# A transformer block on one core: first loads reordered, norms in pairs, the first probabilities turned amid the second scores, context tiles in the order of use

## The chip, the cores and the metric

The kernel runs on one core of one Trainium2 chip. Its engines are TensorE (PE), VectorE (DVE), ScalarE (ACT), GpSimd (POOL) and SyncE (SP), which here only issues DMA transfers. The metric is the device time of one execution in microseconds, the median of several runs.

## What is computed

The input `x` is 8 batches of 64 tokens with 512 channels; a context `ctx` has 512 rows of 512 for each batch. Three residual steps follow each other, each on a layer norm of `x`:

```python
x = x + xattn(layernorm(x), ctx)      # cross attention
x = x + attn(layernorm(x))            # delta rule, FIR filters, gates
x = x + ffn(layernorm(x))             # 8 routed experts (top 2) and 2 shared ones
```

The change touches the first step alone:

```python
def xattn(inputs, context):
    gate_signal = context @ Wg + bg
    attn = softmax(gate_signal @ inputs^T, over the context rows)
    return (attn^T @ context) @ Wo + bo
```

## The kernel before

Everything is float32. The 512 tokens are NT = 4 tiles of 128 tokens, two batches in each; the 512 channels are DC = 4 chunks of 128. The program is written by hand for each engine: what stands in an engine's block is its queue, in that order, and engines meet at semaphores (`wait_ge`). Nothing reorders it.

Instead of multiplying the context by `Wg`, the kernel multiplies the normed tokens by it (`transform`), so that the scores are one product of the transformed tokens with the turned context. `bg` then adds one number per token (`c0s`, VectorE's `tensor_tensor_reduce`), which the exponential's bias takes in.

**SP's queue** loads, in this order: `x[0]`, `consts` (identity, masks and small tables in one block), `x[1]` to `x[3]`, `wgT` (1 MB), `cols`, `rows`, `tickets`, `bgrow`, then for each tile the turned context `ctxT` (2 MB, for the scores) and the context `ctx` (2 MB, for the values), with `wox` (1 MB) after tile 1. All go through one DMA queue. Only then does SP wait, for the first turned values (`oT_done`), and loads `wqkv` over tile 0 of the ring.

**VectorE** does for each tile `begin_norm(t)` (statistics, mean and variance, variance plus eps; GpSimd then raises it to a power) and `end_norm(0, t)` (four small steps of a reciprocal root, and the write of `xn[t]`), interleaved: the beginning of tile t+1 comes before the end of tile t. Then come the four products for `c0s`, `keep_transform` (PSUM to `yT`), `x + bo`, and `score_bias` (maximum over a row of scores and two small steps).

**TensorE** waits for `consts`, runs two 512-column matmuls on them for warm-up (`keep_warm`, the result is not used), transposes tile 0 (`transpose_tile`, waits for `xn_ready`), runs a third, and then does `transform(0)` in two halves of 8 matmuls each around the transposes of tile 1; then a set of transposes and a transform of the tile before, in turn. Then come `scores(0)`, `scores(1)`, `turn_probs(0)` and, for each tile, `values`, `turn_probs` of the next, `project` of the one before, `scores` of the one after next, `turn_values`. One transform is 16 matmuls, one tile of scores or values 8, a set of transposes 4; each float32 matmul stands in the trace as two records.

**ScalarE** copies the transposed tiles to `xnT`, makes `exponentials(0)` and `exponentials(1)`, and then for each tile copies the turned probabilities from PSUM to `probsT_b` (`pT_ready`, which `values` waits for), makes the exponential of the next and scales the values.

After the cross attention come the projections `wqkv` of the second step (line 613 on). Its convolutions, FIR filters and delta rule take until about 240 us, and the experts the rest.

The lines that matter, in the profile's numbers: L499 warm-up, L512 transposes of the normed tile, L523 transform, L547 scores, L557 `turn_probs`, L569 values, L579 `turn_values`, L590 `project`, L613 the first projections; on VectorE L1371 to L1373 `begin_norm`, L1365 to L1368 the root, L1379 the write of `xn`, L1398 the products, L1392 `keep_transform`, L1415 to L1417 `score_bias`, L1427 the reciprocal in `normalise`, which waits for the exponential; on ScalarE L1080 the copy to `xnT`, L1090 the exponential, L1099 the copy of the turned probabilities, L1106 the values.

## Time and profile before

| what | us |
|---|---|
| median of 3 runs | 448.68 (448.63 to 451.23) |
| profiled execution | 448.59 |
| its span, first to last instruction | 446.8 |
| TensorE busy | 429.9 |
| VectorE busy | 307.0 |
| ScalarE busy | 175.5 |
| DMA | 92.41 MB, mean 207 GB/s |

The span is what the trace shows; the execution's own time is 1.8 us longer, for what lies around it. Times in the trace count from the span's start. Busy shares are a mean over stages with different limits; what ends a stage is read from the chain of waits, which follows the last instruction back to what released each step.

### The profile page before, as it was taken

Reading aid. Unit: us, or ns where it says so; the run is one execution under the profiler, and the core shown is the slowest. Engines: PE = TensorE matmul, PEld = TensorE weight load, DVE = VectorE, ACT = ScalarE, POOL = GpSimd, SP = SyncE. Lnnn points to the kernel's source line nnn. Section 1 sums busy time; section 2 is a strip of 40 time slices with the busy share of each in tenths; the row PEclk is TensorE's granted clock in tenths of the full one; section 3 lists DMA queues with packets and bytes.
Section 4 is the critical chain, followed back from the end, with each engine's and each line's share of the span. In section 5 each row is a group of like instructions: output and inputs, shape, how many; then the busy total and the mean of one; then the engine's idle time right before and its main releaser. Section 6 shows DMA issues by size and latency. Waiting matters only on the chain.

```text
span 446.8 us, 8180 instructions
## 1 busy us (share of the span) xinstructions
PE 429.9 (96%) x3184; PEld 287.5 (64%) x3184; DVE 307.0 (69%) x572; ACT 175.5 (39%) x235; POOL 73.8 (17%) x78
## 2 busy tenths in 40 slices
PE   5998999999999999999999999999999999999996
PEld 2953345744445756688865398884457788888872
DVE  5541235698889899886658966510475899999965
ACT  1102111387752211022223243110337778888730
POOL 1000000000023700228631100155100000000061
PEclk9999999999998999999779999999999999999999
DMA  8999959836212530065000200044989999999545
GB/s 318 433 428 425 425 244 321 266 92 187 102 32 94 161 91 9 4 266 208 3 0 0 96 0 2 24 166 85 269 305 389 347 373 412 377 397 396 223 135 170
DMA packets 17937, 92.41 MB, mean 207 GB/s; under 512 B 3424, under 2 KB 5104, under 8 KB 10736
## 3 DMA queue, kind: packets, MB, share of 16 engines
q1 hardware_dynamic: 14880, 78.82, 47.4%
q10 hardware_dynamic: 1488, 8.93, 5.8%
q0 software_dynamic: 1536, 4.20, 2.9%
q8 instruction: 23, 0.38, 0.3%
q14 instruction: 10, 0.08, 0.1%
HBM read 82.25 MB, written 12.08 MB: 211 GB/s over the span
## 4 chain that ended last, share of the span: by engine, by line
PE 82%; DVE 9%; SPq 2%; DMA 2%; issue 1%; ACT 1%; POOL 1%; DVEq 0%; ACTq 0%
PE bank L921 34%; PE bank L735 8%; PE bank L660 6%; PE bank L686 4%; PE bank L569 3%; PE bank L523 3%; PE bank L547 3%; PE bank L590 3%; PE bank L499 2%; SPq L333 2%; DVE part L1496 2%; PE bank L711 2%; PE bank L897 2%; DVE x L1712 1%; PE bank L712 1%
## 5 line engine op out<-in xcount | busy, mean ns | idle before, releaser
L1496 DVE SCALAR_TENSOR_TENSOR part<-ring,cols,part 128x504 f32<-128x504 f32 (+13 forms) x64 | 42.0, 715 | 0.1
L735 PEld LDWEIGHTS bank<-ring 64*64 64x64 f32 x960 | 33.4, 140 | 10.2 <-issue 8.8
L735 PE MATMUL bank<-ring 64*64 64x64 f32 (+1 forms) x960 | 37.8, 230 | 0.8 <-issue 0.7
L686 PE MATMUL bank<-xnT,ring 128*128 128x512 f32 (+1 forms) x96 | 37.7, 544 | 0.7 <-ACT xnT L1080 0.7
L427 POOL TENSOR_TENSOR small<-small 128x1 f32<-128x1 f32 (+2 forms) x12 | 12.1, 1005 | 134.6 <-DVE small L1373 73.6
L660 PE MATMUL bank<-early,ring 128*32 128x512 f32 (+15 forms) x512 | 33.3, 402 | 0.3 <-DVE early L1515 0.3
L1496 DVE SCALAR_TENSOR_TENSOR ring<-bank,cols,ring 128x504 f32<-128x504 f32 (+2 forms) x36 | 26.3, 733 | 5.1 <-ACT ring L1128 4.1
L686 PEld LDWEIGHTS bank<-xnT,ring 128*128 128x128 f32 x96 | 17.6, 190 | 17.2 <-issue 14.5
L1262 ACT ACTIVATE rows<-bank 128x512 f32<-128x512 f32 x19 | 11.4, 598 | 39.5 <-PE bank L921 39.5
L660 PEld LDWEIGHTS bank<-early,ring 128*32 128x32 f32 x512 | 14.5, 112 | 15.2 <-issue 11.2
L436 POOL TENSOR_TENSOR ring<-ring,consts 128x256 f32<-128x256 f32 x20 | 15.8, 815 | 46.8 <-DVE ring L1628 32.5
L1693 DVE TENSOR_TENSOR w1a<-early,w1a 128x2048 fp32r<-128x2048 f32 x7 | 16.0, 2288 | 10.3 <-issue 10.3
L1218 ACT ACTIVATE ring<-bank 128x256 f32<-128x256 f32 x20 | 7.7, 384 | 34.6 <-PE bank L735 34.0
L499 PE MATMUL bank<-consts 128*128 128x512 f32 x24 | 16.2, 801 | 4.8 <-DMA consts<-masks_in 4.8
L1768 DVE TENSOR_TENSOR hTa<-rows,bank 128x512 f32<-128x512 f32 x15 | 10.3, 687 | 13.0 <-PE bank L921 12.9
L486 POOL TENSOR_TENSOR small<-small 128x1 f32<-128x1 f32 x1 | 0.2, 195 | 111.1 <-DMA ys<-yout 111.1
L921 PE MATMUL bank<-xe,hTs 128*128 128x512 f32 x72 | 17.9, 398 | 0.6 <-DVE hTs L1867 0.6
L921 PE MATMUL bank<-w3a,xgT 128*128 128x512 f32 x72 | 18.0, 398 | 0.0
L1693 DVE TENSOR_TENSOR w3a<-early,w3a 128x2048 fp32r<-128x2048 f32 x7 | 16.0, 2287 | 2.8 <-ACT w3a L1194 2.8
L1194 ACT ACTIVATE w1a<-early 128x2048 fp32r<-128x2048 f32 x7 | 13.4, 1908 | 11.2 <-DMA early<-wffn_in 11.2
L921 PE MATMUL bank<-w1a,xgT 128*128 128x512 f32 x72 | 17.5, 392 | 0.0
L569 PE MATMUL bank<-ring,early 128*64 128x512 f32 x64 | 14.6, 599 | 1.9 <-ACT early L1099 1.9
(256 smaller groups left out, 903.5 us busy)
## 6 DMA issues: line engine op xcount, KB each, us to landing
early<-wffn_in SPq DMA_DIRECT2D x21, 1024.0 KB, 7.4
ring<-ctxT_in SPq DMA_DIRECT2D x4, 2048.0 KB, 26.3
ring<-ctx_in SPq DMA_DIRECT2D x4, 2048.0 KB, 30.7
raw1b<-wffn_in SPq DMA_DIRECT2D x6, 1024.0 KB, 9.8
raw3b<-wffn_in SPq DMA_DIRECT2D x6, 1024.0 KB, 8.9
raw2b<-wffn_in SPq DMA_DIRECT2D x6, 1024.0 KB, 7.9
ring<-firw_in SPq DMA_DIRECT2D x4, 1024.0 KB, 4.9
xs<-zeros_in ACTq DMA_DIRECT2D x1, 3840.0 KB, 13.9
```

Of the source, the lines that this page charges most:

```text
L436: pool.tensor_tensor(by_tile(lts[l][:, h]), by_tile(mt[:, h]), spread_half(HF_L1 + 1 + l), ALU.mult).then_inc(S["lt_ready"], 1)
L499: pe.matmul(dst, ident, consts[:, 0:512], start=True, stop=True)
L523: last = pe.matmul(bank[2 + t % 2][:, c * P:(c + 1) * P], wgT[:, e, c * P:(c + 1) * P], xnT[:, e, t * P:(t + 1) * P], start=(e == 0), stop ...
L547: last = pe.matmul(bank[5 + t % 2][b * L:(b + 1) * L, :], yT[:, c, t * P + b * L:t * P + (b + 1) * L], ctxT[t][:, b, c, :], start=(c == 0) ...
L569: last = pe.matmul(bank[t % 2][b * L:(b + 1) * L, :], probsT_b[:, t % 2, k * P + b * L:k * P + (b + 1) * L], ctx[t][:, b, k, :], start=(k ...
L590: last = pe.matmul(bank[2 + t % 2][:, :], oT_b[:, t % 2, c * P:(c + 1) * P], wox[:, c, :], start=(c == 0), stop=(c == DC - 1))
L660: last = pe.matmul(d, firw[h][:, g, m, :], v, start=(m == 0), stop=(m == FW - 1))
L686: last = pe.matmul(bank[QB[g % 3]][:, ts], wqkv[:, j, c, h * P:(h + 1) * P], xnT[:, c, ts], start=(c == 0), stop=(c == DC - 1))
L735: last = pe.matmul(dst[s, d], left[s, L * t:L * (t + 1)], right(s, t), start=True, stop=True)
L921: last = pe.matmul(dst, lhsT, rhs, start=(first and n == 0), stop=(final and n == len(terms) - 1))
L1496: return dve.scalar_tensor_tensor(out=d, in0=s, scalar=w, in1=d, op0=ALU.mult, op1=ALU.add)
L1693: dve.tensor_tensor(split[:, 1, :], raw[:, :] if r % 2 else raw, split[:, 0, :].bitcast(F32), ALU.subtract).then_inc(w_lo[which], 1)
```

## The change

It has five parts, all in the first step of the block.

1. **First loads.** `x[0]` and `x[1]` come first, then the identity alone (128 columns of `consts`), `wgT` in two halves (the array is laid out on the host so that each half, two of the four output chunks, is contiguous), `x[2]` and `x[3]`, and then the rest of `consts` with the other tables. The semaphores follow: `ld_ident` for the identity, `ld_wg[i]` for a half, one `ld_tables` of 80 for the five tables. `iota`'s semaphore is merged into `ld_late`, whose loads VectorE waited for at the same place.
2. **Warm-up.** TensorE waits for `x[0]` in place of `consts`, and runs three 256-column matmuls on `x[0]` before the first transposes and one after, in place of two and one of 512 columns.
3. **Norms in pairs.** VectorE begins tiles 0 and 1, ends tiles 0 and 1, then the same with 2 and 3.
4. **The turn.** `turn_probs(0)` stands between the two halves of `scores(1)`, and ScalarE copies the turned probabilities of tile 0 before it makes the exponential of tile 1.
5. **Context tiles.** Turned 0, turned 1, context 0, turned 2, context 1, `wox`, turned 3, context 2, context 3.

TensorE's queue from its start to the first probabilities. `bank0` and `bank1` take transposes (4 matmuls, L512 before, L528 now), `bank2` and `bank3` transforms, `bank5` and `bank6` the scores of tiles 0 and 1, `bank7` warm-ups and turned probabilities, `bank0<-ring,early` is `values(0)`. Before:

```order
L499 MATMUL bank7<-consts 128x512 x2
L512 MATMUL bank0<-consts,part 128x128 x4
L499 MATMUL bank7<-consts 128x512
L523 MATMUL bank2<-xnT,part 128x128 x8
...
L547 MATMUL bank5<-ring,early 64x512 x8
L547 MATMUL bank6<-ring,early 64x512 x8
L557 MATMUL bank7<-consts,early 128x128 x4
L569 MATMUL bank0<-ring,early 64x512 x8
```

and now:

```order
L547 MATMUL bank7<-x 128x256 x3
L528 MATMUL bank0<-consts,part 128x128 x4
L549 MATMUL bank7<-x,consts 128x256
L540 MATMUL bank2<-xnT,part 128x128 x8
...
L567 MATMUL bank5<-ring,early 64x512 x8
L567 MATMUL bank6<-ring,early 64x512 x4
L578 MATMUL bank7<-consts,early 128x128 x4
L567 MATMUL bank6<-ring,early 64x512 x4
L590 MATMUL bank0<-ring,early 64x512 x8
```

The warm-ups shrink and read `x`, and the four transposes of the first probabilities move up by four score matmuls.

ScalarE's queue at the same place (`bank5` and `bank6` are scores, `bank7` turned probabilities, `bank0` values). Before:

```order
L1090 ACTIVATE early,small<-bank5,small 128x512
L1090 ACTIVATE early,small<-bank6,small 128x512
L1099 ACTIVATE early<-bank7 128x512
L1106 ACTIVATE early<-bank0,small 128x512
L1099 ACTIVATE early<-bank7 128x512
```

and now:

```order
L1112 ACTIVATE early,small<-bank5,small 128x512
L1120 ACTIVATE early<-bank7 128x512
L1112 ACTIVATE early,small<-bank6,small 128x512
L1127 ACTIVATE early<-bank0,small 128x512
L1120 ACTIVATE early<-bank7 128x512
```

The copy of the first turned probabilities no longer stands behind the exponential of tile 1.

The diff:

```diff
--- before.py
+++ after.py
@@ -132,7 +132,8 @@
         ident = masks[:, M_ID, :]
         ctxT = [ring[:, t, 0:4096].rearrange("p (b c k) -> p b c k", b=PAIR, c=DC) for t in range(NT)]
         ctx = [ring[:, t, 4096:8192].rearrange("p (b c d) -> p b c d", b=PAIR, c=TK // P) for t in range(NT)]
-        wgT, wox, xn = part[:, 0], part[:, 1], part[:, 2]
+        wox, xn = part[:, 1], part[:, 2]
+        wgT = part[:, 0].rearrange("p c n -> p (c n)").rearrange("p (i e n) -> p i e n", i=2, e=DC)
         yT = early[:, 0, :].rearrange("p (c n) -> p c n", c=DC)
         probs_b = early[:, 1, 0:1024].rearrange("p (i n) -> p i n", i=2)
         probsT_b = early[:, 1, 1024:2048].rearrange("p (i n) -> p i n", i=2)
@@ -230,7 +231,8 @@
 
 
         ld_x = [sem(f"ld_x{t}") for t in range(NT)]
-        ld_masks, ld_rows, ld_wg, ld_wox, ld_wqkv = (sem(n) for n in ("ld_masks", "ld_rows", "ld_wg", "ld_wox", "ld_wqkv"))
+        ld_ident, ld_tables, ld_wox, ld_wqkv = (sem(n) for n in ("ld_ident", "ld_tables", "ld_wox", "ld_wqkv"))
+        ld_wg = [sem(f"ld_wg{i}") for i in range(2)]
         ld_ctxT = [sem(f"ld_ctxT{t}") for t in range(NT)]
         ld_ctx = [sem(f"ld_ctx{t}") for t in range(NT)]
         ld_w1, ld_w3, ld_w2 = ([sem(f"ld_w{n}_{i}") for i in range(2)] for n in (1, 3, 2))
@@ -239,7 +241,7 @@
         st_y = [sem(f"st_y{i}") for i in range(2)]
         ld_yg = [sem(f"ld_yg{t}") for t in range(NT)]
         zeroed, placed = sem("zeroed"), sem("placed")
-        ticketed, ld_late, ld_iota = (sem(n) for n in ("ticketed", "ld_late", "ld_iota"))
+        ticketed, ld_late = (sem(n) for n in ("ticketed", "ld_late"))
         w_hi = [sem(f"w_hi{i}") for i in range(3)]
         w_lo = [sem(f"w_lo{i}") for i in range(3)]
         ld_firw = [sem(f"ld_firw{h}") for h in range(H)]
@@ -304,20 +306,34 @@
 
         @block.sync
         def _(sp):
-            sp.dma_start(x[:, 0], x_in[0]).then_inc(ld_x[0], 16)
-            sp.dma_start(consts[:], masks_in).then_inc(ld_masks, 16)
-            for t in range(1, NT):
+            for t in range(2):
                 sp.dma_start(x[:, t], x_in[t]).then_inc(ld_x[t], 16)
-            sp.dma_start(wgT, wg_in).then_inc(ld_wg, 16)
-            sp.dma_start(cols[:], cols_in).then_inc(ld_wg, 16)
-            sp.dma_start(rows[:], rows_in).then_inc(ld_rows, 16)
-            sp.dma_start(tickets[:], tickets_in).then_inc(ld_rows, 16)
-            sp.dma_start(bgrow, bg_in).then_inc(ld_rows, 16)
-            for t in range(NT):
+            sp.dma_start(consts[:, 0:P], masks_in[:, 0:P]).then_inc(ld_ident, 16)
+            for i in range(2):
+                sp.dma_start(wgT[:, i], wg_in[:, i]).then_inc(ld_wg[i], 16)
+            for t in range(2, NT):
+                sp.dma_start(x[:, t], x_in[t]).then_inc(ld_x[t], 16)
+            sp.dma_start(consts[:, P:], masks_in[:, P:]).then_inc(ld_tables, 16)
+            sp.dma_start(cols[:], cols_in).then_inc(ld_tables, 16)
+            sp.dma_start(rows[:], rows_in).then_inc(ld_tables, 16)
+            sp.dma_start(tickets[:], tickets_in).then_inc(ld_tables, 16)
+            sp.dma_start(bgrow, bg_in).then_inc(ld_tables, 16)
+
+            def load_turned(t):
                 sp.dma_start(ring[:, t, 0:4096], ctxT_in[t]).then_inc(ld_ctxT[t], 16)
+
+            def load_context(t):
                 sp.dma_start(ring[:, t, 4096:8192], ctx_in[t]).then_inc(ld_ctx[t], 16)
-                if t == 1:
-                    sp.dma_start(wox, wox_in).then_inc(ld_wox, 16)
+
+            load_turned(0)
+            load_turned(1)
+            load_context(0)
+            load_turned(2)
+            load_context(1)
+            sp.dma_start(wox, wox_in).then_inc(ld_wox, 16)
+            load_turned(3)
+            load_context(2)
+            load_context(3)
             sp.wait_ge(S["oT_done"], 1)
             sp.dma_start(ring[:, 0, 0:6144], wqkv_in).then_inc(ld_wqkv, 16)
             sp.dma_start(ring[:, 0, 6144:8192], wod_in).then_inc(ld_wqkv, 16)
@@ -398,7 +414,7 @@
             load_up(0, 0)
             load_up(1, 1)
             sp.wait_ge(S["rout_done"], 1)
-            sp.dma_start(iota, iota_in).then_inc(ld_iota, 16)
+            sp.dma_start(iota, iota_in).then_inc(ld_late, 16)
             sp.wait_ge(ticketed, 16 * TOPK * NT)
             for i in range(2):
                 sp.dma_start(late[:, i, :], info[bass.ds((last_group + (GB - 1 + i)) * P, P)]).then_inc(ld_late, 16)
@@ -502,7 +518,7 @@
 
                 pe.wait_ge(S["xn_ready"], layer * NT + t + 1)
                 if layer == 0 and t == 0:
-                    pe.wait_ge(ld_masks, 16)
+                    pe.wait_ge(ld_ident, 16)
                 if t >= 2:
                     pe.wait_ge(S["xnT_ready"], layer * NT + t - 1)
                 elif layer == 1:
@@ -514,21 +530,23 @@
 
             def transform(t, lo=0, hi=DC):
 
-                pe.wait_ge(ld_wg, 32)
+                if t == 0:
+                    pe.wait_ge(ld_wg[lo // 2], 16)
                 pe.wait_ge(S["xnT_ready"], t + 1)
                 if t >= 2:
                     pe.wait_ge(S["yT_ready"], t - 1)
                 for c in range(lo, hi):
                     for e in range(DC):
-                        last = pe.matmul(bank[2 + t % 2][:, c * P:(c + 1) * P], wgT[:, e, c * P:(c + 1) * P],
+                        last = pe.matmul(bank[2 + t % 2][:, c * P:(c + 1) * P], wgT[:, c // 2, e, c % 2 * P:(c % 2 + 1) * P],
                                          xnT[:, e, t * P:(t + 1) * P], start=(e == 0), stop=(e == DC - 1))
                 if hi == DC:
                     last.then_inc(S["y_done"], 1)
 
-            pe.wait_ge(ld_masks, 16)
-            keep_warm(bank[7][:, :], 2)
+            pe.wait_ge(ld_x[0], 16)
+            for _ in range(3):
+                pe.matmul(bank[7][:, 0:2 * P], x[:, 0, 0:P], x[:, 0, 0:2 * P], start=True, stop=True)
             transpose_tile(0, 0)
-            keep_warm(bank[7][:, :], 1)
+            pe.matmul(bank[7][:, 0:2 * P], ident, x[:, 0, 0:2 * P], start=True, stop=True)
             transform(0, 0, 2)
             transpose_tile(0, 1)
             transform(0, 2, DC)
@@ -537,17 +555,20 @@
                 transform(t - 1)
             transform(NT - 1)
 
-            def scores(t):
+            def scores(t, lo=0, hi=DC):
                 pe.wait_ge(S["yT_ready"], t + 1)
+                if t == 0:
+                    pe.wait_ge(ld_tables, 80)
                 pe.wait_ge(ld_ctxT[t], 16)
                 if t >= 2:
                     pe.wait_ge(S["exp_done"], t - 1)
-                for c in range(DC):
+                for c in range(lo, hi):
                     for b in range(PAIR):
                         last = pe.matmul(bank[5 + t % 2][b * L:(b + 1) * L, :],
                                          yT[:, c, t * P + b * L:t * P + (b + 1) * L], ctxT[t][:, b, c, :],
                                          start=(c == 0), stop=(c == DC - 1))
-                last.then_inc(S["s_done"], 1)
+                if hi == DC:
+                    last.then_inc(S["s_done"], 1)
 
             def turn_probs(t):
                 pe.wait_ge(S["exp_done"], t + 1)
@@ -592,8 +613,9 @@
                 last.then_inc(S["proj_done"], 1)
 
             scores(0)
-            scores(1)
+            scores(1, 0, DC // 2)
             turn_probs(0)
+            scores(1, DC // 2, DC)
             for t in range(NT):
                 values(t)
                 if t + 1 < NT:
@@ -1091,13 +1113,12 @@
                                accum_out=sm[:, t:t + 1]).then_inc(S["exp_done"], 1)
 
             exponentials(0)
-            exponentials(1)
             for t in range(NT):
                 act.wait_ge(S["pT_done"], t + 1)
                 if t >= 2:
                     act.wait_ge(S["pv_done"], t - 1)
                 act.activation(probsT_b[:, t % 2, :], bank[7][:, :], ACT.Copy).then_inc(S["pT_ready"], 1)
-                if 1 <= t < NT - 1:
+                if t < NT - 1:
                     exponentials(t + 1)
                 act.wait_ge(S["pv_done"], t + 1)
                 act.wait_ge(S["rs_ready"], t + 1)
@@ -1379,12 +1400,12 @@
                 dve.tensor_scalar(xn[:, t, :], x[:, t, :], mv[:, t, 0:1], rq[:, t:t + 1], ALU.subtract,
                                   ALU.mult).then_inc(S["xn_ready"], 1)
 
-            for t in range(NT):
-                dve.wait_ge(ld_x[t], 16)
-                begin_norm(t)
-                if t >= 1:
-                    end_norm(0, t - 1)
-            end_norm(0, NT - 1)
+            for first in range(0, NT, 2):
+                for t in (first, first + 1):
+                    dve.wait_ge(ld_x[t], 16)
+                    begin_norm(t)
+                for t in (first, first + 1):
+                    end_norm(0, t)
 
             def keep_transform(t):
 
@@ -1392,7 +1413,7 @@
                 dve.tensor_copy(yT[:, :, t * P:(t + 1) * P],
                                 bank[2 + t % 2][:, :].rearrange("p (c n) -> p c n", c=DC)).then_inc(S["yT_ready"], 1)
 
-            dve.wait_ge(ld_rows, 48)
+            dve.wait_ge(ld_tables, 80)
             dve.wait_ge(S["xn_ready"], NT)
             for t in range(NT):
                 after(dve, dve.tensor_tensor_reduce(out=bgprod, in0=xn[:, t, :], in1=bgrow, scale=1.0, scalar=0.0,
@@ -1400,11 +1421,11 @@
                       S["c0_ready"])
                 if t == 1:
                     keep_transform(0)
-            dve.wait_ge(ld_masks, 16)
+            dve.wait_ge(ld_ident, 16)
             dve.tensor_copy(ident_r[:], ident[:, 0:24]).then_inc(S["identr_ready"], 1)
             for t in range(1, NT):
                 keep_transform(t)
-            dve.wait_ge(ld_rows, 48)
+            dve.wait_ge(ld_tables, 80)
             for t in range(NT):
                 dve.wait_ge(S["xn_ready"], NT)
                 do(dve.tensor_tensor(x[:, t, :], x[:, t, :], rows[:, R_BO:R_BO + D], ALU.add))
@@ -1895,8 +1916,7 @@
                 if t < 2:
                     low_routed(1, 1, t)
                 if t == NT - 2:
-                    dve.wait_ge(ld_iota, 16)
-                    dve.wait_ge(ld_late, 32)
+                    dve.wait_ge(ld_late, 48)
                     for i in range(2):
                         dve.tensor_scalar(picks[:, i, :], iota, late[:, i, 0:1], late[:, i, 1:2], ALU.is_equal,
                                           ALU.mult).then_inc(S["late_ready"], 1)
@@ -1977,7 +1997,7 @@
         "x_in": a["x"].reshape(NT, P, D),
         "ctx_in": by_tile,
         "ctxT_in": byT,
-        "wg_in": chunks(a["L0_xattn_Wg"].T).reshape(P, DC, D),
+        "wg_in": chunks(a["L0_xattn_Wg"].T).reshape(P, DC, 2, D // 2).transpose(0, 2, 1, 3),
         "wox_in": chunks(a["L0_xattn_Wo"]).reshape(P, DC, D),
         "wqkv_in": np.concatenate([chunks(a[f"L0_attn_W{s}"].T) for s in "vkq"], axis=1),
         "wod_in": chunks(a["L0_attn_Wo"].T),
```

## Rows read from the trace of the kernel before

**Rows 1.** The page, part 1: TensorE's busy time, share, instructions.

```profile
PE 429.9 (96%) x3184; PEld 287.5 (64%) x3184; DVE 307.0 (69%) x572; ACT 175.5 (39%) x235; POOL 73.8 (17%) x78
```

**Rows 2.** The chain of waits, 0 to 110 us: start, us, what.

```profile
4.82 3.78 PE bank L499 x4
...
10.98 1.78 PE bank L523 x16
...
19.00 0.44 PE bank L512 x4
...
26.58 7.04 PE bank L547 x32
...
36.08 3.65 PE bank L569 x16
39.73 0.59 PE bank L557 x4
...
52.09 3.58 PE bank L547 x16
...
76.45 3.45 PE bank L613 x16
```

**Rows 3.** The timeline, 3 to 10 us: start, us, engine, line [idle before].

```profile
3.28 0.69 DVE L1371 BATCH_NORM_STATS2 small<-x 128x6 f32<-128x512 f32 x1 [3.28 <-DMA x<-x_in]
...
5.15 0.46 SPq L315 DMA_DIRECT2D early<-bg_in  x1
5.44 0.69 DVE L1371 BATCH_NORM_STATS2 small<-x 128x6 f32<-128x512 f32 x1 [1.06 <-DMA x<-x_in]
...
6.46 0.15 DVE L1365 TENSOR_TENSOR small<-small 128x1 f32<-128x1 f32 x1
...
7.25 0.55 DVE L1379 TENSOR_SCALAR part<-x,small 128x512 f32<-128x512 f32 x1
7.71 0.69 DVE L1371 BATCH_NORM_STATS2 small<-x 128x6 f32<-128x512 f32 x1
...
8.39 1.06 PE L512 MATMUL bank<-consts,part 128*128 128x128 f32 x4
...
9.49 0.60 ACT L1080 ACTIVATE xnT<-bank 128x512 f32<-128x512 f32 x1 [7.50 <-PE bank L512]
```

**Rows 4.** Busy time by window, with the granted clock third from the end.

```profile
0.00:11.00 11.00, 6.18 (x12) 2.95 (x13) 6.10 (x23) 1.88 (x2) 2.05 (x9) 1.00 0.87 320
...
137.00:140.20 3.20, 3.20 (x58) 2.73 (x58) 3.06 (x9) 1.26 (x2) 0.64 (x1) 0.50 0.02 5
...
218.80:229.10 10.30, 10.30 (x79) 6.56 (x77) 3.80 (x8) 2.57 (x3) 4.33 (x4) 0.50 0.01 2
```

**Rows 5.** DMA: a window (last column GB/s); issues (KB each, us to landing); `wqkv`'s issue.

```profile
3.00:4.50 1.50, 0.00 (x0) 0.00 (x0) 1.03 (x3) 0.00 (x0) 0.00 (x0) 1.00 0.95 368
...
early<-bg_in SPq DMA_DIRECT2D x1, 256.0 KB, 6.8
...
ring<-wqkv_in SPq DMA_DIRECT2D x1, 3072.0 KB, 17.5
...
44.52 0.33 SPq L322 DMA_DIRECT2D ring<-wqkv_in  x1
```

**Rows 6.** The timeline around the first probabilities, 30 to 36 us.

```profile
30.28 0.69 DVE L1415 TENSOR_REDUCE small<-bank 128x1 f32<-128x512 f32 x1 [0.20 <-PE bank L547]
...
32.21 0.16 DVE L1427 RECIPROCAL small<-small 128x1 f32<-128x1 f32 x1 [0.84 <-ACT early L1090]
...
35.44 0.59 ACT L1099 ACTIVATE early<-bank 128x512 f32<-128x512 f32 x1
```

**Rows 7.** Ring loads: issue ns and first and last issue, then us to landing.

```profile
L317 SPq DMA_DIRECT2D ring<-ctxT_in x4: 442/443/654, 5.7 to 9.3; - x4
...
DMA to landing us min/median/max: 11.2/26.3/40.5
...
L318 SPq DMA_DIRECT2D ring<-ctx_in x4: 442/450/2105, 6.4 to 9.8; - x4
...
DMA to landing us min/median/max: 16.6/30.7/44.9
```

## The prediction

> **What bounds the kernel now.** I read the page first, then the chain of waits from the start to 110 us, then the timeline of the first 37 us, then the DMA queue. The page has TensorE busy for 96% of the span [rows 1]. In the stretch that the change touches the chain is TensorE almost alone [rows 2]: after the load of `consts` it runs through the warm-up matmuls (from 4.82), the transform (from 10.98) and the scores (26.58 to 33.62), leaves TensorE once for 2.46 us (33.62 to 36.08, for VectorE's bias, ScalarE's exponential and copy), and is back on it until 100 us. So there are two things to win: a start of the useful TensorE work ahead of 10.98, and the hole before 36.08. What is won is kept only if nothing that is timed independently, a transfer or the clock, comes in between.
>
> The granted clock matters too. Its column shows 1.00 over the first 11 us [rows 4], but the durations there say half speed: tile 0's four transposes span 1.06 us [rows 3], later four take 0.44 to 0.59 [rows 2]. The transform has full speed from its first matmul (16 records in 1.78 us at 10.98, and 32 of the scores' wider ones in 7.04) [rows 2]. So TensorE is at 1.2 GHz from 4.82 to about 10.7 us, and at 2.4 GHz after. The column names two more stretches at 0.50, 137.0 to 140.2 and 218.8 to 229.1 [rows 4].
>
> **First loads.** Before, `x[1]` stands behind a `consts` of 473.5 KB, and VectorE waits 1.06 us for it, until 5.44 [rows 3]. Now it is second. `x[0]` had landed at 3.28, and 256 KB more at 368 GB/s [rows 5] are 0.7 us: `x[1]` lands near 4.0. VectorE ends `begin_norm(0)` near 4.40 (three steps after 3.28, as it needs 1.02 from 5.44 to 6.46 for the same three) and goes on at once: what began at 5.44 begins at 4.40. The identity (64 KB, in rows of 512 B) comes next. Its cost is bounded by nothing and by the wait of TensorE for the whole `consts`, until 4.82 [rows 2]: even at 4.82 it is ahead of its use at 6.8, so I take zero. The two halves of `wgT`, 1.05 MB at the same rate from 4.2, are there at 5.6 and 7.0; `x[2]` and `x[3]` at 7.8 and 8.5. These two used to be early; now VectorE wants them at 7.9 and 8.9. That is the tightest place of the start, but TensorE does not want tile 2 before 13.6, so 1.5 us of lateness would be hidden.
>
> The tables behind them are the same bytes at the same place of the queue. They share one semaphore now, of which `bgrow` lands last, at 5.15 + 6.8 = 11.95 [rows 3, 5]. VectorE's products want it at 12.6. TensorE's new wait on it, with all scores queued behind, comes at 25. Both cost zero. If VectorE's cover of 0.6 fails, `keep_transform(0)` is late by that, which TensorE wants only after 17 us.
>
> **Norms in pairs.** VectorE takes 1.02 us from `begin_norm(1)` to the first step of the next reciprocal root, 0.79 from there to the write of `xn` (6.46 to 7.25), and 0.55 for that [rows 3]. With `begin_norm(1)` from 4.40 the root starts at 5.42 and `xn` of tile 0 is written from 6.21 to **6.76**, against 7.80 before. Tile 1 is ready at 8.0 (0.46 after 6.21 the next root starts, as `begin_norm` did at 7.71), then come two beginnings (2 x 1.02) and two ends (1.25 each): tile 2 at about 11.3, tile 3 at 12.5. TensorE wants them at 11.4, 13.6 and 17.6. GpSimd's power is asked for a full beginning ahead of its use. Cost zero.
>
> **TensorE's start.** Before: two warm-up matmuls of 512 columns from 4.82 in 3.78 us, the transposes, a third warm-up until 10.98 [rows 2]. Now three of 256 columns run on `x[0]` from 3.3. Each is half of one that took 1.7 to 1.9, so the three take 2.6 to 2.8 us and end at 6.0, and TensorE idles 0.8 us until `xn`. The transposes at half speed are 2 x 0.44 = 0.88, to 7.7; the fourth small warm-up 0.85, to 8.5, beside ScalarE's copy (it began 1.10 after the first transpose and took 0.60 [rows 3], so it is done at 8.5). The transform may start at **8.6**, still at 1.2 GHz. When the clock rises decides what this is worth. I take the moment of the trace, 10.7, since from 6.8 on TensorE is full in both kernels. From 8.6 to 10.7 half speed does 1.05 us of the 1.78 of the first half transform; 0.73 remain, which ends it at 11.4. Before it ended at 10.98 + 1.78 = 12.76. **Gain 1.35 us.** From there the same transposes and transforms follow without a wait, to first scores at 25.2 in place of 26.58.
>
> **The turn.** Before, in a row after the second scores: the first probabilities are transposed, VectorE reduces the second scores, ScalarE makes the second exponential and only then copies the transposed probabilities (at 35.44 [rows 6]), until 36.08: 2.46 us. After, ScalarE copies first, and TensorE turns the probabilities amid the second scores. The scores take 7.04 / 2 = 3.52 a tile, 1.76 a half. From the end of the first scores (26.58 + 3.52 = 30.10) to the reciprocal that waits for the exponential (32.21 [rows 6]) are 2.1 us. TensorE has 1.76 of cover and **stalls for 0.34**. The transposes cost 0.44 to 0.59 [rows 2], I take 0.52. The copy of 0.59 [rows 6] lies under the other half. So 0.34 + 0.52 in place of 2.46: **gain 1.60**. Late next is the exponential of tile 1: 2.1 us after its scores, under `values(0)`, 3.65 [rows 2], so free by 1.5.
>
> **Context tiles.** The first turned tile lands at 5.7 + 11.2 = 16.9, the last at 9.3 + 40.5 = 49.8, the last context at 9.8 + 44.9 = 54.7 [rows 7]; 6.5 tiles of 2 MB from the first to the last turned make 5.06 us a tile. In the old order the last turned one comes 2.3 us ahead of its use at 52.09 [rows 2]; with all of it 3 us earlier it would cost 0.7. In the new order it comes sixth and a half, at 44.7, and is wanted at 49.1. Context 2 comes at 49.8 and is wanted one scores and one set of transposes later than that, at 53.2. The first ones are wanted at 25.2 (there at 16.9) and 28.7 (there at 22). So the order costs nothing and gives nothing by itself; it guards 0.7. `wqkv` is issued 3 us earlier than at 44.52, but behind the same bytes, so it lands at 44.5 + 17.5 = 62 as before [rows 5], wanted at 73.5 in place of 76.45 [rows 2]. SP's queue has no new wait.
>
> **Sum.** 1.35 + 1.60 = 2.95 us. The profiled execution took 448.59 us for a span of 446.8; less 2.95 that is 445.64. The median of the runs, 448.68, is 0.09 above it: I predict **445.7 us**, 0.66% less. Past 100 us the chain is made of engines that wait for each other and of SP's issues behind ScalarE's `silu_done`, all relative to what came before, so I carry the gain to the end. About 1%, 4.5 us, is what a measurement of this kernel can tell from no change.
>
> **Rivals.** *The clock rises later.* For it: TensorE's new start is broken by an idle 0.8 us, while before the rise in the trace it had been busy since 4.82. Against: from 6.8 on it is full. The shorter low stretch is 3.2 us [rows 4]; a rise that much later, at 13.9, loses 1.6: gain 1.35, 447.3. The Trainium skill, page "TensorE: Matmul & The Clock Gate", Part 4, says that a transpose doesn't count as TensorE being busy for the clock gate; by it the broken start holds even less that counts, which would be this rival's 447.3. The rise at 10.7 followed a run with one set of transposes in it, so the trace neither bears the rule out nor excludes it. *The clock stays low for long*, the one that ends slower. Its place is TensorE's start; with the 10.3 us of the longer stretch [rows 4] added it costs 5.15: 450.9. It decides from a rise at 16.6 on (10.7 + 2 x 2.95). *The clock rises earlier*, as the first matmul is 1.5 us earlier: at 9.2, another 0.75, 444.9. *The later low stretches change.* TensorE's thin stretches come to them 3 us earlier; one could be 3.2 us longer, shorter or gone, 1.6 either way: 444.1 or 447.3. The three runs, 448.63 to 451.23, say that something of that size happens. *The new order doesn't do what it says*: if `x[1]` still comes at 5.44, `xn` is ready at 7.8 and the first half transform ends near 11.9, 0.5 less gain: 446.2.
>
> **How the numbers follow.** Forecast 0.52; clock later 0.13, low for long 0.03, clock earlier 0.10, later stretches shorter 0.07 or longer 0.07, order without effect 0.05, rest 0.03. All but the long one lie in 444.1 to 447.3; with 0.4 for the unsure terms (2.6 to 2.8, and a stall between 0 and 0.6) the range is **443.7 to 447.8**. Faster by over 1% means under 444.2: half of the shorter stretches, and an earlier clock together with another case, 0.10. Slower by over 1%, above 453.2: 0.02. Within: 0.88.
>
> **What would show it.** First matmul at 3.3; `xn` of tile 0 at 6.8; first transform at 8.6, its records falling to half their duration near 10.7; first scores at 25.2; a wait of 0.3 before the first probabilities are transposed and none before the first values, at 33.1; no wait for a ring load; the low stretches where they were. I am wrong if the transform has long records until 14, if the first values wait for a DMA or for ScalarE, or if 3 us are won at the first values and not at the end.

## The result

The changed kernel took 444.03 us in the median of 5 runs (440.33 to 446.29), beside 448.95 us of the kernel before (5 runs, 448.63 to 451.23): a ratio of 0.9882, with a 95% interval of 0.9848 to 0.9917. On the kernel before that is 5.3 us, where 3.0 were forecast. In the same executions the mean granted clock of the changed kernel was 1.000, 0.992, 0.992, 0.985 and 0.985 at 440.33, 442.49, 444.03, 445.20 and 446.29 us. So one kernel comes at several clocks, and the text below gives means over all executions of a kernel, with their standard error (the ratios leave out executions over 1.5% above the kernel's fastest, five of the twelve of start_and_order). Over the study these are 449.22 +- 0.17 us (the 128 executions of the experiments) for the kernel before and 444.28 +- 0.42 (23) for the changed one: 4.9 us.

The page of the changed kernel's profiled execution (440.33 us) has no low clock at all in its 40 slices:

```profile
span 438.5 us, 8185 instructions
PE 422.5 (96%) x3186; PEld 283.9 (65%) x3186; DVE 306.8 (70%) x572; ACT 175.5 (40%) x235; POOL 73.7 (17%) x78
...
PEclk9999999999999999999999999999999999999999
```

Its chain of waits over the first 40 us (start, us, what) answers to [rows 2]:

```profile
0.70 2.73 DMA x<-x_in
3.45 0.70 DVE small L1392
...
6.26 0.56 DVE part L1400
...
6.86 1.13 PE bank L528 x4
8.02 0.61 ACT xnT L1102
...
8.76 2.02 PE bank L540 x16
...
24.71 3.61 PE bank L567 x16
...
30.36 0.66 PE bank L578 x4
31.02 1.87 PE bank L567 x8
32.88 3.43 PE bank L590 x16
```

The steps are where the prediction put them: transposes at 6.86 (6.8 forecast), transform at 8.76 (8.6), first scores at 24.71 (25.2), a short wait before the first probabilities are transposed, first values at 32.88 (33.1), against 36.08 in [rows 2]. That is 3.2 us, but as the sum of two misses that partly cancel: the start won 1.9 (forecast 1.35) and the turn 1.3 (forecast 1.60). And the gap grows later. The same pieces far down the two chains, first the kernel before:

```profile
214.02 1.15 PE bank L735 x32
...
234.04 3.44 PE bank L897 x8
```

and the changed one:

```profile
210.16 1.15 PE bank L757 x32
...
225.73 3.44 PE bank L919 x8
```

The changed kernel is 3.9 us ahead at the first of these pieces and 8.3 at the second. In between lies the low stretch of before, 218.8 to 229.1 [rows 4], which this execution does not have. So 4.4 us of the 8.26 between the two profiled executions are that stretch. Another 0.6 to 0.9 are the one at 137: the gap is 3.0 us at 128 and 3.8 at 146. The question was whether the change has to do with that.

### The profile page after: what moved, and what is told of

Its sections match the earlier page's. It is cut to its first block, busy times and chain, and to the rows that moved or that the text cites. A ratio compares the mean times of both kernels' runs of the same rounds, so it can differ in the third digit from the quotient of the medians.

```text
span 438.5 us, 8185 instructions
## 1 busy us (share of the span) xinstructions
PE 422.5 (96%) x3186; PEld 283.9 (65%) x3186; DVE 306.8 (70%) x572; ACT 175.5 (40%) x235; POOL 73.7 (17%) x78
## 4 chain that ended last, share of the span: by engine, by line
PE 80%; DVE 11%; DMA 2%; SPq 2%; issue 1%; ACT 1%; POOL 1%; DVEq 0%; ACTq 0%
PE bank L943 35%; PE bank L757 8%; PE bank L682 5%; PE bank L708 4%; PE bank L540 3%; PE bank L590 3%; PE bank L611 3%; PE bank L567 3%; SPq L349 2%; DVE part L1517 2%; PE bank L733 2%; PE bank L919 2%; DVE x L1733 1%; PE bank L635 1%; PE bank L734 1%
## 5 line engine op out<-in xcount | busy, mean ns | idle before, releaser
L1517 DVE SCALAR_TENSOR_TENSOR part<-ring,cols,part 128x504 f32<-128x504 f32 (+13 forms) x64 | 41.9, 712 | 0.1
L757 PEld LDWEIGHTS bank<-ring 64*64 64x64 f32 x960 | 31.8, 134 | 8.6 <-issue 7.0
L757 PE MATMUL bank<-ring 64*64 64x64 f32 (+1 forms) x960 | 36.2, 224 | 0.8 <-issue 0.7
L1283 ACT ACTIVATE rows<-bank 128x512 f32<-128x512 f32 x19 | 11.4, 598 | 40.5 <-PE bank L943 40.5
L943 PE MATMUL bank<-xe,hTs 128*128 128x512 f32 x72 | 17.9, 397 | 0.8 <-DVE hTs L1888 0.8
L1215 ACT ACTIVATE w1a<-early 128x2048 fp32r<-128x2048 f32 x7 | 13.4, 1909 | 11.7 <-DMA early<-wffn_in 11.7
L943 PEld LDWEIGHTS bank<-xe,hTs 128*128 128x128 f32 x72 | 13.3, 188 | 4.6 <-issue 1.7
L943 PEld LDWEIGHTS bank<-w1a,xgT 128*128 128x128 f32 x72 | 13.5, 188 | 3.3 <-issue 0.5
```

Source lines behind the costliest of these rows:

```text
L757: last = pe.matmul(dst[s, d], left[s, L * t:L * (t + 1)], right(s, t), start=True, stop=True)
L943: last = pe.matmul(dst, lhsT, rhs, start=(first and n == 0), stop=(final and n == len(terms) - 1))
L1215: act.activation(splits[which][r % 2][:, 0, :], raw[:, :] if r % 2 else raw, ACT.Copy).then_inc(w_hi[which], 1)
L1517: return dve.scalar_tensor_tensor(out=d, in0=s, scalar=w, in1=d, op0=ALU.mult, op1=ALU.add)
```

## The experiments

All were timed beside the kernel before, on four chips in turn; the kernel before had 448.8 to 449.9 us on them. "Mean" is compared with all 128 executions of it, the ratio with those on the same chip. "Low" is the mean time at half clock after TensorE's start, worked out as 2 x (1 - mean clock) x span and averaged over the executions. The last column is an estimate of what is left at equal clock. A straight line through the 128 executions has 388 us for each unit of mean clock (0.43 us for each us of low time). Each execution is corrected by it, and the difference is taken to the kernel before on the same chip; a minus is faster.

| kernel | mean us | n | low us | ratio (interval) | at equal clock, us |
|---|---|---|---|---|---|
| before | 449.22 +- 0.17 | 128 | 12.7 | | |
| changed, three times | 444.28 +- 0.42 | 23 | 9.4 | 0.9882, 0.9913 (0.9878 to 0.9949), 0.986 (0.9814 to 0.9906) | -3.9 +- 0.3 and -3.7 +- 0.5 (second and third time) |
| turn_only | 448.17 +- 0.51 | 12 | 12.0 | 0.9979 (0.9945 to 1.0013) | -1.0 +- 0.3 |
| start_only | 448.56 +- 0.55 | 12 | 11.6 | 0.9994 (0.9954 to 1.0034) | -0.4 +- 0.4 |
| order_only | 448.43 +- 0.49 | 12 | 12.0 | 0.9997 (0.9964 to 1.003) | -0.1 +- 0.2 |
| turn_and_order | 446.45 +- 0.51 | 12 | 11.7 | 0.9946 (0.9911 to 0.998) | -2.0 +- 0.3 |
| start_and_order | 447.14 +- 0.70 | 12 | 12.1 | 0.9922 (0.988 to 0.9963) | -1.5 +- 0.3 |
| old_context_order | 450.53 +- 0.49 | 12 | 15.1 | 1.0045 (1.0008 to 1.0082) | +0.5 +- 0.3 |
| norms_as_before | 446.21 +- 0.49 | 12 | 12.2 | 0.9954 (0.9918 to 0.999) | -2.6 +- 0.3 |
| hole_filled | 446.85 +- 0.53 | 12 | 8.9 | 0.9959 (0.9924 to 0.9994) | -0.4 +- 0.4 |
| start_order_hole_filled | 446.93 +- 1.22 | 6 | 11.0 | 0.9896 (0.9843 to 0.9949) | -2.0 +- 0.6 |
| before_filled | 453.10 +- 0.71 | 12 | 9.5 | 1.0088 (1.0044 to 1.0131) | +5.5 +- 0.3 |
| after_filled | 448.66 +- 0.75 | 12 | 7.0 | 0.9999 (0.9959 to 1.0038) | +2.1 +- 0.3 |
| late_warmup_one | 443.61 +- 0.91 | 8 | 5.3 | 0.9835 (0.9795 to 0.9875) | -2.9 +- 0.4 |
| late_warmup_two | 445.05 +- 0.57 | 6 | 5.9 | 0.9897 (0.9851 to 0.9942) | -1.7 +- 0.3 |

**Does the time follow the clock?** The two kernels unchanged, for more executions.

> The kernel before, unchanged, to see each execution's granted clock beside its time. The profile of the changed kernel has no low stretch after TensorE's start, and its five executions had mean clocks of 1.000, 0.992, 0.992, 0.985 and 0.985 at 440.3, 442.5, 444.0, 445.2 and 446.3 us. Theory A (the work won is the 3 us forecast, and the rest is the two later low stretches, which come or not by how the clock's moments fall on the work): the kernel before shows different clocks too, or always 0.985, and in either case its executions at 0.985 are 448.6 to 449.2, about 3 us over the changed kernel's at 0.985. Theory B (the change itself made the later part 5 us faster, whatever the clock): the executions of this kernel at a higher clock, if there are any, are still near 448.

> The changed kernel, unchanged, for five more executions and a second profile. Theory A: times between 440 and 446.5 us that fall as the mean clock rises, those at 0.985 near 445.5, those at 1.000 near 440.3; first values again at 32.9 us. Theory B: the times do not follow the clock, and the later part is short in every one.

The kernel before shows all clocks too, from 0.979 to 0.999, and its time follows them: 452.2 us at 0.979 (6 executions), 449.4 at 0.985 (43), 446.9 at 0.992 (16), 443.9 at 0.999 (2). The five runs known before the change, 448.63 to 451.23, were a narrow draw. At the same clock the changed kernel is 2.9 us faster at 0.985 (446.4, 7 executions) and 3.8 at 0.992 (443.1, 9). Theory A holds for that part. But its low time is 3.3 +- 1.0 us shorter in the mean, about 1.4 us of time by the line above, which A put down to luck.

**The parts alone.** The turn, and the start (loads, warm-ups, paired norms), each with the old order of the context tiles:

```diff
 turn_only: before, with
+            scores(1, 0, DC // 2)
             turn_probs(0)
+            scores(1, DC // 2, DC)
 and on ScalarE exponentials(1) after the first copy
```

> The kernel before with the turn alone (first probabilities transposed amid the second scores, ScalarE copies them ahead of the second exponential). In the profile the hole of 2.46 us before the first values shrinks to a wait of 0.35 and the transposes, 0.66: first values at 34.5 in place of 36.08. Theory A: 447.1 us at a clock of 0.985 (1.6 less), and less than that only in executions with a higher clock. Theory B, that the later part gains too: 445 or less at a clock of 0.985.

> The changed kernel with the turn and the order of the context tiles as before, so that the first loads, the warm-up and the paired norms are alone. First transform matmul at 8.75 and first scores between 24.6 and 25.3, as the moment at which the clock rises falls (8.3 in the changed kernel's profile, 10.7 in that of before); the hole of 2.46 is back. Theory A: 447.0 to 447.4 us at a clock of 0.985 (1.3 to 1.7 less). Theory B: 445 or less at 0.985.

By the means, 1.3 +- 0.7 and 1.0 +- 0.7 us under the kernel before on the same chip, neither can be told from what was expected nor from nothing; at equal clock both stay short of it. The chains tell more. The gain is there at the first values (34.64 in turn_only, 34.83 in start_only, against 36.08) and gone one step later. The chain of turn_only:

```profile
34.64 3.43 PE bank L570 x16
38.08 0.59 PE bank L558 x4
38.67 1.81 issue
40.48 3.65 PE bank L547 x16
```

"issue" is a wait for which the profile shows no releaser; the scores that end it wait only for turned tile 2 besides what was long done. By the DMA records that tile landed at 40.0 in the kernel before (issued at 8.3, 31.7 us later), which used it at 40.32, so the slack was 0.3 us. It landed at 40.4 in turn_only, whose scores start at 40.48. start_only waits 2.65 us, until 41.72: there the tile landed only at 41.6. That is a second thing that the prediction did not have. The new start gives SP two more loads to issue ahead of the ring (`wgT` and `consts` in two parts each); the ring's first load went out at 7.8 in place of 5.7, and all of the ring came later.

**The order of the context tiles and the norms**, each put back in the changed kernel:

```diff
 old_context_order: changed kernel, with
+            for t in range(NT):
+                load_turned(t)
+                load_context(t)
+                if t == 1:
+                    sp.dma_start(wox, wox_in).then_inc(ld_wox, 16)
 norms_as_before: changed kernel, with
+            for t in range(NT):
+                dve.wait_ge(ld_x[t], 16)
+                begin_norm(t)
+                if t >= 1:
+                    end_norm(0, t - 1)
+            end_norm(0, NT - 1)
```

> The changed kernel with the context tiles in the old order alone. Turned tile 2 is the sixth transfer of the ring there and landed near 40 us in the runs of the turn alone and of the start alone, whose third scores began at 40.48 and 41.72. Theory 1 (the order of the context tiles carries the whole gain past 37 us): the third scores, at 36.9 in the changed kernel, wait 3.5 us for it and begin at 40.3 to 41, so the time is that of the kernel before, 449 to 450. Theory 2 (my prediction's: the order guards only 0.7 us): 0.7 us above the changed kernel, 445.

> The changed kernel with the norms interleaved as before. x[2] lands at 9.50 there. Theory 1 (the pairs matter because VectorE would wait for x[2] ahead of the end of tile 1's norm): tile 1 is written near 11.8 in place of 8.04, TensorE waits 1.2 us or more before tile 1's transposes, and first scores come at 26 in place of 24.7; about 1.3 us slower than the changed kernel. Theory 2 (my prediction's cost of zero for the norms): no difference at the first scores.

The chain of old_context_order has the wait in full, and the clock falls in it (low from 41.9 to 45.3 by its profile):

```profile
37.61 0.59 PE bank L574 x4
38.20 4.14 issue
42.34 5.11 PE bank L563 x16
```

The wait ends when turned tile 2 lands, at 42.2. The tile took as long as before, but was issued later; here is the ring's line in old_context_order, to be held against 5.7 to 9.3 and 40.5 in [rows 7]:

```profile
L323 SPq DMA_DIRECT2D ring<-ctxT_in x4: 446/466/504, 8.2 to 11.8; - x4
DMA to landing us min/median/max: 11.1/25.6/40.2
```

So of the 4.14 us some 2.2 are the new start's later issue, and the rest is that TensorE comes 2.1 us earlier and had 0.3 of slack. The kernel is 1.3 us slower than the kernel before and 6.3 slower than the changed one: without this part the change is worth nothing. With the norms as before, VectorE's timeline has a wait for `x[2]`, 3.27 us in brackets, ahead of the end of tile 1's norm:

```profile
10.10 0.69 DVE L1392 BATCH_NORM_STATS2 small<-x 128x6 f32<-128x512 f32 x1 [3.27 <-DMA x<-x_in]
```

and its chain:

```profile
12.49 0.66 PE bank L528 x4
13.15 3.07 PE bank L540 x16
```

Tile 1's transposes begin at 12.49 in place of 10.78, and the 16 records after them take 3.07 us in place of 1.79: in that execution the clock fell back at 13.4 for 3.4 us after the wait, and first scores came at 28.17 where 26 was expected. The kernel is 1.9 +- 0.6 us slower than the changed one, where 1.3 were expected, and low time goes from 9.4 to 12.2.

**Is it the late stretches?** Both kernels with four warm-up matmuls (512 columns, result not used) at the places near 137 and 219 us, where TensorE runs many small matmuls:

```diff
             pe.wait_ge(S["bv_ready"], H)
+            keep_warm(bank[0][:, :], 1)
...
+                if 5 <= step < 8:
+                    pe.wait_ge(S["o_ready"], 2)
+                    keep_warm(bank[7][:, :], 1)
```

> The kernel before with four more warm-up matmuls of 512 columns (results not used): one ahead of the key products near 135 us and three amid the last levels of the delta rule, 212 to 220 us, where the clock falls. Theory A (the runs spread because the clock's moments fall differently on thin TensorE stretches, 137 and 219 us): the mean clock is 0.996 or more in nearly all executions, the spread over executions shrinks from 8 us to 3, and the median is 446 to 448, as 5.6 us of low clock are bought off with at most 3.4. Theory B (the spread comes from elsewhere): same spread, 1 to 3 us slower.

> The changed kernel with the same four warm-ups. Theory A: clock 0.996 or more, small spread, and 3.3 to 3.8 us faster than the kernel before with them, which is the change without the clock's later stretches: of the 5.2 us between the means, 1.4 is the clock's luck or pattern. Theory B (the change makes the later part faster by itself): still 5 us faster than the kernel before with the warm-ups.

Not as expected. Low time fell only from 12.7 to 9.5 and from 9.4 to 7.0, the spread stayed, and both kernels got 4 us slower (one of the warm-ups waited 1.45 us for `o_ready`). The difference between them, 4.4 +- 1.0, decides nothing between 3.5 and 5; at equal clock it is 3.4 +- 0.4. The profile of before_filled has a low stretch that the profile of the kernel before has not: 36.6 to 40.0, right after the hole of 2.46 us.

**The hole and the clock.** So the hole of the kernel before was filled, and the remaining combinations run:

```diff
 hole_filled: before, with
             turn_probs(0)
+            keep_warm(bank[4][:, :], 2)
```

> The kernel before with two warm-up matmuls of 512 columns (results not used) in the hole ahead of the first values, where TensorE waits 1.9 us for ScalarE. They take 1.7 us, so no work moves: first values at 36.1 as before. Theory H (in a part of its executions the kernel before loses the clock in or just after that hole, and the change closes the hole, which is where its gain over the forecast comes from): no low stretch near 36 to 40 us, mean low time over the executions 2 to 3 us less than in the kernel before, mean time 0.8 to 1.5 us less. Theory N (the clocks differ for another reason): clocks and times as in the kernel before.

> The kernel before with the turn and the new order of the context tiles. Theory: no wait for turned tile 2, so the 1.5 us of the turn last to the end, and the closed hole lowers the low time by 2 to 3 us: 446.5 to 447.2 in the mean, 2.5 us under the kernel before. Rival (the order gives nothing, as forecast): as the turn alone, 448.2.

> The changed kernel without the turn. Theory: first scores at 24.7 to 25.3, 1.3 us or more won and kept to the end, the hole there as before and with it the clocks of the kernel before: 447.7 to 448.1 in the mean. Rival (the start brings the better clocks): 446.5 or less, with low time as in the changed kernel.

> The kernel before with the new order of the context tiles alone. In the profile of before turned tile 2 lands at about 40 us, just ahead of the third scores at 40.25. All theories: no step waits for a ring load in either order while the steps stand where they were, so the time and the clocks are those of the kernel before, 449.3 in the mean.

Order_only leaves the work of before where it was, and its profiled execution shows the stretch. Busy time by window (granted clock third from the end), order_only:

```profile
33.30:36.60 3.30, 1.41 (x10) 0.72 (x10) 1.17 (x4) 1.26 (x3) 0.00 (x0) 1.00 0.95 395
36.60:40.00 3.40, 3.40 (x12) 0.96 (x10) 0.00 (x0) 0.00 (x0) 0.00 (x0) 0.50 1.06 448
40.00:45.00 5.00, 5.00 (x28) 1.67 (x24) 0.00 (x0) 1.18 (x2) 0.00 (x0) 1.00 1.01 423
```

and hole_filled:

```profile
33.30:36.60 3.30, 3.13 (x14) 1.41 (x14) 1.17 (x4) 1.27 (x3) 0.00 (x0) 1.00 1.02 427
36.60:40.00 3.40, 3.40 (x18) 1.14 (x14) 0.00 (x0) 0.35 (x1) 0.00 (x0) 1.00 1.00 424
```

TensorE is busy 1.41 of 3.3 us ahead of the fall, and 3.13 of 3.3 where it does not fall. Order_only's chain gives the price:

```profile
36.01 5.35 PE bank L579 x16
41.36 0.59 PE bank L567 x4
```

5.35 us for the first values in place of 3.65 [rows 2], 1.7 us, and nothing hides it. Of six profiles of kernels with the open hole two have this stretch (before_filled, order_only), and four have not (before, before_again, start_only, start_and_order). Of the twelve profiles without the open hole none has it there, though old_context_order has one in its own wait. That is a hint and no proof: two of six against none of twelve can be chance. In the two the clock had risen at 9.3 us, in the four at 6.3, 8.4, 9.8 and 10.7, so the moment of the rise may have a part in it. Filling the hole with unused matmuls, which moves no work (first values at 35.95), makes the kernel before 1.9 +- 0.6 us faster than the executions of it on the same chip, and 2.4 +- 0.6 than all 128. Nearly all of that is clock: at equal clock 0.4 +- 0.4 are left. For this run theory H holds in its sign. In size it does not: 2 of 6 times 1.7 us is 0.6 us; the rest came with shorter low time later on (8.9 in place of 12.7 us in all), for which no run shows a reason.

The other runs speak against H. The turn closes the hole, and turn_and_order was expected to lose 2 to 3 us of low time by it. It had 11.7 us. The three kernels that close the hole by the turn (turn_only, turn_and_order, norms_as_before; old_context_order is left out for the low stretch in its own wait) have 12.0 +- 0.7 us in the mean, and the three with the open hole (start_only, start_and_order, order_only) 11.9 +- 0.8. Closing the hole by the turn did not shorten low time; only the whole change did, to 9.4 +- 0.9.

Turn_and_order gains 2.8 +- 0.5 us where 2.5 were expected, start_and_order 2.1 +- 0.7 where 1.3 were (2.3 and 1.7 against the kernel before on the same chip). Both contain the new order, so they can't simply be added up; less order_only's 0.8 they make 4.1 +- 1.0, beside 4.9 for the whole change. At equal clock the same sum is 3.4, beside 3.7 to 3.9. The rival for turn_and_order, that the order gives nothing, would have had 448.2 and is unlikely. Order_only's 0.8 +- 0.5 is no difference by its ratio.

**Once more, and the late stretches.** The same fill in the changed start, the changed kernel a third time, and one or two warm-ups amid the small matmuls near 214 us:

```diff
 late_warmup_one (late_warmup_two: 6 <= step)
+                if 7 <= step < 8:
+                    pe.wait_ge(S["o_ready"], 2)
+                    keep_warm(bank[7][:, :], 1)
```

> The changed kernel, unchanged, as the measure for the three beside it on this chip: 444 to 445 in the mean, first values at 32.8 to 33.6, no low stretch before 130 us, low time 9 to 10 us in the mean against 12.5 of the kernel before.

> The changed kernel without the turn, and with two warm-up matmuls in the hole that is back. The step not yet settled is how much of the turn's gain is moved work (1.5 us) and how much is the clock that the hole costs. Theory H (the hole's clock counts in every kernel that has it): faster than the same kernel with the open hole, which had 447.1, by 0.8 to 2, so 445.1 to 446.3, and 1 to 2 us slower than the changed kernel, which saves the hole too. Theory N: 447.1.

> The changed kernel with one more warm-up matmul of 512 columns ahead of the last spread of weights, near 214 us, where it costs 0.85 us and waits for nothing (the three of the earlier try cost 4.5 us with a wait of 1.5). If the stretch at 217 to 229 can be shortened by that, low time falls by 3 us or more and the mean is about 1 us under the changed kernel's: 443.5. Rival: the stretch comes anyway and the time is 0.85 more.

> The same with two, one each ahead of the last two spreads: costs 1.7 us, low time less by 6 us or more, mean 443.5 to 444.5 if the stretch's price is half of its length; 1.7 us more than the changed kernel if the stretch comes anyway.

After_third repeats the mean (444.2) and the low time (8.6 us). Its profile shows what the start can do. The chain:

```profile
6.83 1.12 PE bank L528 x4
7.94 0.85 PE bank L549 x2
8.80 3.68 PE bank L540 x16
...
26.61 3.61 PE bank L567 x16
...
34.77 3.43 PE bank L590 x16
```

The transform begins at 8.80 as in the other profile, but at half speed: 3.68 us for 16 records in place of 2.02. The clock rose at 13.0 in this execution, and first scores come at 26.61, as in the kernel before (26.58). This is the rival "the clock rises later", in one profile of three; in the other two it rose at 8.3 and 8.1 and the start won 1.9 and 1.3. Of all ten profiles with the new start and its paired norms three rose late (12.2 to 13.0, first scores at 26.23 to 26.61).

This profile also has the low stretches of the kernel before, 3.4 us near 136 and 10.2 near 218. Its execution took 447.62 us, 0.97 less than the profiled one of the kernel before, with first values 1.31 earlier. With the same low stretches nothing beyond the moved work is seen in this pair.

Start_order_hole_filled (446.9 +- 1.2) can't be told from start_and_order (447.1 +- 0.7), nor from the 445.1 to 446.3 of theory H: open. Late_warmup_one had less low time in seven of its eight executions (0.989 or more, five at 0.996 and above) and the lowest median of all, 442.50, but its mean of 443.6 +- 0.9 is not apart from the changed kernel's; in its profiled execution the stretch came anyway, with the warm-up itself at half speed (`215.61 2.00 PE bank L515 x2`). Two warm-ups are no better than one. Both beat the kernel before; whether the one beats the changed kernel stays open.

## Why the prediction was off

- **The turn: right.** Forecast 1.60. From first scores to first values it took 9.50 us in the kernel before and in start_and_order, and 8.17 in turn_only and the changed kernel: 1.33, and 1.5 one step later. The stall of 0.34 was there, and the exponential of tile 1 hidden. The transposes were mis-sized, 0.66 in place of 0.52, and the two halves of the scores took 0.1 more.
- **The start: right in the place, wrong in "I take the moment of the trace, 10.7".** That moment belongs to one execution. In the profiles it was 8.0 to 10.7 with the start of before, and 6.3 to 13.0 with the new one; the gain at the first scores went from 1.9 to nothing. That the forecast 1.35 is near the middle is luck. I had also missed what held the start of before: a weight load of the first transform waited until 10.56 for `cols` (its row in the timeline is `10.56 2.01 PEld L523 LDWEIGHTS bank<-xnT,part 128*128 128x128 f32 x16 [0.98 <-DMA cols<-cols_in]`), so an earlier rise there, 8.0 in turn_only, won nothing: in all seven profiles with that start first scores came at 26.45 to 26.62.
- **First loads: they came later than I worked out.** The halves of `wgT` landed at 7.5 and 8.8, not 5.6 and 7.0, and the identity at 5.9 (6.5 in start_and_order), where I had bounded it by 4.82; TensorE wanted it at 6.8. VectorE got `x[2]` at 9.50, not 7.8. It was all hidden, as said, but `x[2]` only by the pairs: "Cost zero" for the norms was right for the change and blind to what they buy, 1.9 us.
- **Context tiles: mis-sized.** "It guards 0.7" looked at the last turned tile, which has 2.3 us of slack. Turned tile 2 has 0.3. It also took the ring to land as before (first tile at 16.9), while the new start issues it 1.4 to 2.6 us later (first tile at 17.9 to 19.3). Without the new order the changed kernel loses 6.3 us, 4.1 of them in one wait; the rest came with the clock, low from 41.9 and 15.1 us in all.
- **"I carry the gain to the end", with the low stretches where they were: this failed.** I read the clock's stretches as marks of the kernel at fixed places, and gave their change 0.14. They differ from execution to execution. 3.2 us were won at the first values in the profiled execution (forecast 2.95; 2.7 and 1.3 in the other two), and the mean is 4.9 lower. At equal clock the two kernels are 2.9 to 3.9 us apart, so 1 to 2 us come with the shorter low time, 9.4 us in place of 12.7. The sum had that term at nothing. Why it is shorter no run shows: that the change closes a hole after which the clock can fall is a part of the answer at most, as turn_and_order closes it too and keeps its low time.
- **Slower than before** by a long low clock at the start did not happen: the slowest of 23 executions took 447.62 us. (The upper end of the range, 447.3 + 0.4, is 447.7 and not 447.8; nothing hangs on it.)

What stays open: why low time is shorter in the changed kernel and in hole_filled, when TensorE's queue past the cross attention is the same, and whether the difference at equal clock (3.7 to 3.9 us on the same chips) is more than the moved work (1.3 to 3.2 us at the first values of three profiles).

## What to carry to other kernels

When steps are pulled forward, look at the slack of each load in the queue and not of the last one, and at what the new loads ahead of it do to its issue: here one transfer with 0.3 us of slack decided between 1.1% faster and no gain. A hole of two microseconds in TensorE's queue may cost more than its length: in two of six profiles the clock fell right behind it. Two unused matmuls in the hole are a cheap test of that; here they won 1.9 +- 0.6 us in one kernel and nothing that could be measured in another. One profile is one draw of the clock: compare kernels at equal clock, or over a dozen executions.

## What was not expected of the hardware

- The later low stretches lasted between 3.4 and 13.7 us. Their price was not the same everywhere: 10.2 us cost 4.4 us at 219, 3.4 us cost 0.6 to 0.9 at 137, and 3.4 us cost 1.7 at 36.6.
- The clock also fell behind no hole at all. In the kernel before TensorE was busy for the whole 3.4 us ahead of the fall at 218.8, with small matmuls:

```profile
215.40:218.80 3.40, 3.40 (x45) 2.81 (x45) 2.26 (x6) 0.00 (x0) 2.28 (x3) 1.00 0.00 0
218.80:229.10 10.30, 10.30 (x79) 6.56 (x77) 3.80 (x8) 2.57 (x3) 4.33 (x4) 0.50 0.01 2
```

- The clock rose anywhere from 6.3 to 13.0 us into the span, in kernels with the same new start.
- The first load of the routed experts took 4.8 to 5.3 us in most profiles and 7.24 and 6.95 in two (before_again, start_only), with everything around it unchanged. That adds 2 us of its own to an execution.
